# Cross-attention in a decoder layer: exponentials in place, four buffers for the removed scores, queries one step earlier, value products transposed, small operations on GpSimd

## The reference, cut to what matters

```python
q = split_heads(layernorm(x) @ Wq.T + bq)      # 16 heads of 32
k = split_heads(ctx @ Wk.T + bk); v = split_heads(ctx @ Wv.T + bv)
scores = einsum('bhqd,bhkd->bhqk', q, k) / sqrt(32)
top_scores, top_idx = top_k(scores, 32)        # 32 of 722 keys for each query row
w = softmax(top_scores)
out = einsum('bhqk,bhqkd->bhqd', w, v[top_idx])
x = x + out @ Wo.T + bo
```

## Time and profile before

| | |
|---|---|
| time, three runs | 2797.72, 2798.91, 2809.83 us; median 2798.91 |
| span of the profiled execution | 2800.8 us |
| cross-attention, first to last output sum (L1242) | 1206.5 to 2787.4 us |
| busy share of the whole span, PE / DVE / ACT / POOL | 86 / 72 / 50 / 36 % |
| mean granted TensorE clock | 0.88 |

### The profile page before, as it was taken

The page is one execution under the profiler, slowest core; times in us unless marked ns, Lnnn a source line. Parts: engine busy times, 40 slices in busy tenths (PEclk is TensorE's granted clock), DMA queues, the critical chain, the costliest instruction groups (busy, mean ns, idle before and its releaser), DMA issues. The chain is left out here.

```text
span 2800.8 us, 41238 instructions
## 1 busy us (share of the span) xinstructions
PE 2418.1 (86%) x13752; PEld 1992.5 (71%) x13752; DVE 2028.2 (72%) x3897; ACT 1388.0 (50%) x2992; POOL 1016.6 (36%) x912
## 2 busy tenths in 40 slices
PE   3899999999999757898898989888988988988987
PEld 2667767776776536777777868777777877877875
DVE  4544544454454206899898899998989989998996
ACT  3221122112212025667667666766767667676663
POOL 3344334433533112343343343333434433333421
PEclk9787788788878678999999999999999999999987
DMA  4000000000000220010010000000001001000000
GB/s 157 7 18 9 9 17 9 9 9 18 9 9 6 84 86 25 12 28 14 16 28 14 15 20 23 15 20 23 14 16 28 14 16 28 14 16 23 14 1 7
DMA packets 37615, 63.00 MB, mean 22 GB/s; under 512 B 4014, under 2 KB 20542, under 8 KB 37420
## 3 DMA queue, kind: packets, MB, share of 16 engines
q1 hardware_dynamic: 35836, 56.28, 6.7%
q0 software_dynamic: 1584, 4.30, 0.5%
HBM read 53.99 MB, written 6.55 MB: 22 GB/s over the span
## 5 line engine op out<-in xcount | busy, mean ns | idle before, releaser
L1208 DVE MATCH_REPLACE8 ca_W<-ca_top,ca_W 128x722 f32<-128x722 f32 (+1 forms) x624 | 553.5, 894 | 0.0
L1199 DVE MAX8 ca_top<-ca_W 128x8 f32<-128x722 f32 (+1 forms) x624 | 536.4, 898 | 2.6
L855 POOL TENSOR_TENSOR ca_E<-ca_E,ca_S 128x722 f32<-128x722 f32 (+1 forms) x208 | 357.6, 1740 | 308.6 <-ACT ca_S L1060 308.5
L955 PE MATMUL ca_pO<-ca_V,ca_PT 128*128 128x64 f32 (+1 forms) x2496 | 343.1, 293 | 76.8 <-ACT ca_ctxT L1099 76.5
L955 PEld LDWEIGHTS ca_pO<-ca_V,ca_PT 128*128 128x128 f32 (+1 forms) x2496 | 331.1, 205 | 103.8 <-ACT ca_PT L1082 75.6
L837 POOL TENSOR_TENSOR ca_KL<-ca_K,ca_KH 128x384 fp32r<-128x384 f32 (+1 forms) x128 | 114.2, 893 | 496.5 <-ACT ca_KH L1053 496.5
L618 PE MATMUL sa_pq<-sa_V,sa_E 101*100 101x33 f32 x1536 | 258.9, 355 | 29.2 <-POOL sa_E L341 27.8
L618 PEld LDWEIGHTS sa_pq<-sa_V,sa_E 101*100 101x100 f32 x1536 | 257.2, 287 | 30.0 <-issue 30.0
L383 ACT ACTIVATE sa_V<-sa_pp 100x512 f32<-100x512 f32 x48 | 29.2, 608 | 461.1 <-PE sa_pp L90 410.7
L845 POOL TENSOR_TENSOR ca_cL<-ca_raw,ca_cH 128x768 fp32r<-128x768 f32 (+1 forms) x64 | 110.6, 1728 | 332.8 <-ACT ca_cH L1036 332.8
L1187 DVE MAX8 ca_top<-ca_S 128x8 f32<-128x722 f32 (+1 forms) x208 | 181.2, 901 | 54.3 <-ACT ca_S L1077 48.7
(11 more groups left out here) (193 smaller groups left out, 5252.1 us busy)
## 6 DMA issues: line engine op xcount, KB each, us to landing
ca_raw<-in_ctxT SPq DMA_DIRECT2D x32, 384.0 KB, 3.7
ca_raw<-in_ctxT SPq DMA_DIRECT2D x32, 338.0 KB, 3.0
sa_xin<-in_x SPq DMA_DIRECT2D x16, 200.0 KB
sa_xres<-in_x SPq DMA_DIRECT2D x16, 200.0 KB
x_scratch<-sa_x SPq DMA_DIRECT2D x16, 200.0 KB
ca_xin<-x_scratch SPq DMA_DIRECT2D x16, 200.0 KB
out<-ca_x SPq DMA_DIRECT2D x16, 200.0 KB
sa_E<-in_WQ SPq DMA_DIRECT2D x12, 256.0 KB, 13.5
```

The source lines that it names most:

```text
L855: pool.tensor_tensor(E[r][0:t.rows, :], E[r][0:t.rows, :], S[r][0:t.rows, :], ALU.subtract).then_inc(p_ready, 1)
L955: last = pe.matmul(out, PT[:, k, 0:t.rows], rhs, start=k == 0, stop=k == KC - 1)
L1199: n_of[t.i] = order.mark(dve.max(eight, w[rows, :]))
L1208: ins = dve.match_replace(w[rows, :], eight, (w if k else S[r])[rows, :], REMOVED)
```

## The change

All of it is in `cross_program`:

- `exps` writes its exponentials over the scores, in `S`, and so waits until VectorE's first MATCH_REPLACE8 has read them (`removed`); `exps_left` works in `W` in place. `E` is gone, and `W` has four buffers for two.
- The shift (minus the scaled maximum) moves from VectorE to GpSimd (`shifts`, at the head of GpSimd's step, ahead of the subtractions), 1/Z too (`weights`, as a power), and the low part of the queries (`query_low`, at the end of step 5).
- The queries are copied and split by ScalarE at the end of step 5.
- `values` loads 32 columns of V and streams the transposed weights, a block for each head, so that the result stands already transposed in `pO`; a further product writes 1/Z beside it. `normalise`, `output_T` and `place_output` of ScalarE go. In their place ScalarE copies both parts of a group of heads (`keep_output`, five a batch) and GpSimd multiplies them (VectorE for the rest tile, in step 0).
- No work is put off to the next step. y, x2T and f stand behind the first `weights_T`, and the late slices ahead of the first `values`.
- The next batch's x is normalised in step 3 for step 4.

```diff
-        W = [sb(f"W{r}", [128, KV]) for r in range(2)]
+        W = [sb(f"W{r}", [128, KV]) for r in range(RING)]
...
+            def shifts(tb, tp, t):
+                r, rows = ring(t, tp), slice(0, t.rows)
+                pool.wait_ge(peaked, tb.count(NT, t.i + 1))
+                settle(pool)
+                pool.tensor_scalar(shift[rows, r:r + 1], top[r][rows, 0:1], -SCALE, None,
+                                   ALU.mult).then_inc(shift_ready, 1)
...
+                pool.tensor_tensor(S[r][rows, :], S[r][rows, :], W[r][rows, :], ALU.subtract).then_inc(p_ready, 1)
+                need(pool, o_mm, parts_done(ob, Tile(oi)))
+                pool.wait_ge(z_ready, tb.count(NT, t.i + 1))
+                pool.tensor_tensor(rZ[rows, r:r + 1], Z[rows, r:r + 1], minus_one[rows, :], ALU.pow).then_inc(rz_ready, 1)
...
-                if t.i == 0:
-                    pe.wait_ge(q_lo, tb.count(5, 5))
+                if t.i == 0 or t.rest:
+                    pe.wait_ge(q_lo, tb.count(5, 5 if t.rest else 4))
...
+                for _, cols, to, g, q in t.blocks():
+                    pe.matmul(pO[to:to + DH, DEN + at + q.start:DEN + at + q.stop],
+                              rZ[:, r:r + 1].broadcast_to((128, DH)), ident[:, cols], start=True, stop=True)
...
-                    last = pe.matmul(out, PT[:, k, 0:t.rows], rhs, start=k == 0, stop=k == KC - 1)
+                    for _, cols, to, g, q in t.blocks():
+                        last = pe.matmul(pO[to:to + DH, NUM + at + q.start:NUM + at + q.stop],
+                                         V[tp][:, k, 128 * g + to:128 * g + to + DH], PT[:, k, cols],
+                                         start=k == 0, stop=k == KC - 1)
...
             def exps(tb, tp, t):
                 r, rows = ring(t, tp), slice(0, t.rows)
+                act.wait_ge(removed, tb.count(NT, t.i + 1))
+                act.wait_ge(shift_ready, tb.count(NT, t.i + 1))
+                act.activation(S[r][rows, :], S[r][rows, :], ACT.Exp, bias=shift[rows, r:r + 1],
+                               scale=SCALE).then_inc(e_ready, 1)
...
-                                dve.reciprocal(rZ[rows, r:r + 1], Z[rows, r:r + 1]).then_inc(rz_ready, 1)
...
+                        if k == 2 and s == 0 and prev:
+                            dve.wait_ge(ot_ready, b.count(GROUPS, -1))
+                            dve.wait_ge(o_kept, b.count(GROUPS, 0))
+                            rest = [chunks(NR[3 * DH:128, i, 0:4 * REST], 4) for i in range(2)]
+                            dve.tensor_tensor(ctxT[3 * DH:128, :, T - REST:T], rest[0], rest[1],
+                                              ALU.mult).then_inc(ot_ready, 1)
```

More of the change, by code:

```diff
@@ L775, in tiles_at, with parts_done, group_of @@
             return cur, last, coming
[L777 to L781, removed]
+        def parts_done(b, t, before=False):
+            return b.count(PARTS, 2 * t.i if before else min(2 * t.i + 2, PARTS))
+        def group_of(t):
+            if t.rest:
+                return GROUPS - 1
+            return t.g if t.t == 2 else None
         def slices(s, part, b, par, tiles, nxt):
@@ L851, in body @@
                     cur, last, coming = tiles_at(s, b, par, tiles, prev, nxt)
[L852 to L856, removed]
+                    for x in cur:
+                        shifts(*x)
+                    for x in last:
+                        weights(*x)
                     if s == 2 and prev:
@@ new lines, in values @@
+                settle(pe)
+                if t.rest:
+                    n = t.rows
+                    pe.matmul(pO[3 * DH:128, DEN:DEN + n], rZ[0:n, r:r + 1].broadcast_to((n, DH)), ident[0:n, 0:n],
+                              start=True, stop=True)
+                    for g in range(4):
+                        at = NUM + REST * g
+                        for k in range(KC):
+                            last = pe.matmul(pO[3 * DH:128, at:at + REST], V[tp][:, k, 128 * g + 3 * DH:128 * g + 128],
+                                             PT[:, k, REST * g:REST * g + REST], start=k == 0, stop=k == KC - 1)
+                    last.then_inc(o_mm, 1)
+                    return
@@ L967, in body @@
                     cur, last, coming = tiles_at(s, b, par, tiles, prev, nxt)
+                    if coming:
+                        score(*coming[0])
+                    for x in slices(s, 0, b, par, tiles, nxt):
+                        project(*x)
+                    if last:
+                        weights_T(*last[0])
                     if s == 1 and prev:
-                        pe.wait_ge(ot_ready, b.count(NT, 0))
+                        pe.wait_ge(ot_ready, b.count(GROUPS, 0))
                         for c in range(CC):
@@ L1015, in body @@
                         ins.then_inc(q_mm, 1)
-                    if s != 5 and last:
-                        output_T(*last[0])
+                    if len(last) > 1:
+                        values(*last[1])
             each_batch(pe, body)
```

272 lines of the change are left out of this document (129 added, 143 removed).

## The result

The changed kernel takes 2996.19 us (2994.85 to 2996.87), the kernel before on the same chip 2804.37: ratio 1.067, interval 1.0634 to 1.0705. It is slower by 192 us. The profiled execution's span is 2994.4 us, 193.6 more than before.

The account below looks back on a forecast made before the run. VectorE (92% busy) and TensorE (89%) were nearly full, their mutual waits deciding. Steps summed to 115.5 us a batch, 117.0 with clock, 10.2 above 106.8; over 15 batches 2954, so 2952 us, range 2880 to 3030 (55%).

Parts of the forecast that it names:

- VectorE's own pace: VectorE's cross-stage work without waits on other engines, after the change: 93.9 us a batch, about 80% busy.
- The fast rival: VectorE decides because TensorE runs far ahead and old waits vanish: 98.4 us a batch, 2675 us; 17%.
- Where it would wait: VectorE for scores copy (steps 1, 4, 6), f, rest copy; TensorE 4 us each for subtraction (1, 4), query halves (6).
- The steps: Seven parts of a cross-stage batch, 0 to 6; foretold 13.5 to 19.9 us each, sum 115.5.
- The walk: Queue-by-queue timing of a batch's seven steps from VectorE's first MAX8: 115.5 us, 117.0 with the clock, against 106.8 before.
- Clock: TensorE's new idle stretches in steps 1, 4 and 6 lower its clock: 0.5 us each.
- The way into step 4: GpSimd's queue from step 3 into 4: context low part done 3.4, first weights 7.15 us into step 4.
- Values: TensorE's narrow value products: 1.65 us a tile with change-over, 3.0 for the rest tile.
- 106.2 us a batch: Rival that gains and waits cancel: bare pace, half the walk's extra and the clock, 2800 us; 6%.
- the low prices: Rival: the walk with values 1.0, rest 2.55, query halves 0.6, no clock: 111.0 us a batch, 2864 us; 12%.
- GpSimd's prices: Per operation on GpSimd: query half 0.96 us, shift 0.2, power 0.55, subtraction 1.74.
- In-place exponentials at nothing: Exponentials waiting for first replacements delay ScalarE 0.8 us a step, hidden since first weights come later; uncovered, 5.6 a batch.

Follow-up runs that it names:

- e9: Kernel before with four W buffers, exponentials still out of place (E 4, W 4, S 2 buffers): 2801.07 us against 2803.06, ratio 0.9998.
- e5: Changed kernel with the low query halves back on VectorE, in step 6 behind its first replacement: 2943.32 us, ratio 1.0511.
- e3: Changed kernel with y, x2T and f again at the head of TensorE's steps and late slices again behind the second transposition: 2935.67 us, ratio 1.0481.
- e7: Changed kernel with the edits of e3 and e5 together: 2890.06 us, ratio 1.0329.
- e10: Changed kernel with exponentials out of place (E 4, W 4, S 2) and the second scores copy ahead of the second weights copy: 2997.70 us, ratio 1.0687.
- e8: Kernel before with in-place exponentials and four W buffers, nothing else: 2944.81 us, ratio 1.0565.
- e12: e11 with query product in step 4, high halves in step 5, low halves on GpSimd again, second score ahead of first values: 2879.05 us, ratio 1.0245.
- e11: e7 with step 6's first score behind its V slice, several ScalarE and GpSimd reorderings, and exponentials out of place: 2900.29 us, ratio 1.0348.

## Why the prediction held

Forecast 2952 us, measured 2996.19. The mechanism was the one named, and the waits came where they were foretold; that the sum of a batch came within 2 us was in part luck, since errors of several us cancelled. By its steps:

- **VectorE's own pace.** Foretold 93.9 us a batch and 80% busy, measured 93.6 and 79%. The W waits went and the small work went, as priced. None of it reached the time. The fast rival made 98 us of old waits its argument, and half of it has its answer in e9, where the W waits go and the time stays. They were not a cost of their own but the place where VectorE met the pace of the rest. The other half, the waits for the scores copy, grew from 46.8 to 231.7 us.
- **Where it would wait.** Foretold: scores copy in steps 1, 4 and 6, f in 4, rest copy in 0, and on TensorE 4 us each for the subtraction (1 and 4) and the halves (6). Measured: 4.6, 5.3 and 5.15 us on TensorE, and VectorE's waits in the places named; the one small miss is step 4, where f alone does nearly all (3.7 of 4.0 us a batch).
- **The steps.** Foretold 16.8, 17.0, 15.0, 15.1, 19.9, 13.5, 18.2, sum 115.5 and 117.0 with the clock; measured 17.8, 18.9, 15.0, 15.0, 18.4, 12.9, 21.1, sum 119.0. The walk counts from the first MAX8, and step 6 has only one; on its scale steps 5 and 6 took 13.5 and 20.4. Times 15 batches the 2.0 us are 30 of the 40 us by which the profiled execution lies above 2954. Four terms pull against each other in it:
  - *Clock, mis-sized.* I gave 1.5 us a batch. Mean clock fell from 0.95 to 0.90. The lower clock costs the first transposition 0.65 in steps 1 and 4, y 4.70 - 3.05 = 1.65 in step 1, f 0.81 in step 4, the first score 1.96 - 1.1 = 0.86 and the V slice 4.05 - 2.9 = 1.15 in step 6: 5.8 us, and more in the long kind of step 0 (clock 0.70). In step 1 that is 2.3 us, more than the miss of 1.9, in step 6 2.0 of the miss of 2.2.
  - *The stall of the loop, put at nothing.* It is 2.6 to 3.2 us in every second batch, and the walk has no term for it, since its steps were read off a batch that does not have it. So the foretold 16.8 of step 0 is neither the 15.3 of the short kind nor the 21 of the long one, only near their mean.
  - *The way into step 4, mis-sized.* I had GpSimd busy with the context piece until 3.4 and the first weights at 7.15. In the batch shown GpSimd is through with it 0.9 us behind VectorE's first MAX8 of step 4, and TensorE starts the first transposition at 1859.83: 4.7 us into the step, 2.5 earlier than foretold. This is why step 4 came out 1.5 below the walk in spite of the clock.
  - *Values, mis-sized the other way.* 28 passes took 0.97 to 1.32 us where I took 1.65, and the rest tile's 50 passes 1.82 (1922.40 to 1924.22 in TensorE's timeline) where I took 3.0. With five values products and the rest on the chain of the slow steps, my prices were 3 to 4 us a batch too high. This and the way into step 4 hid most of the clock and of the stall. By the Trainium skill, "TensorEngine Tiling (Array Packing)", Overview and Tiling Modes, I had estimated 0.7 to 1.0 with a drain on each side. The trace agrees with strips that run side by side: the time follows the wider of a tile's two blocks (the last section has the numbers). It shows no drain to be priced.
- **Slips in the rivals.** 106.2 us a batch gives 2792 and not 2800, and the low prices as listed take 5.1 off 115.5, which gives 110.4 and not 111.0. Neither moves a rival into another's range.
- **GpSimd's prices.** Halves 4.52 us for four beside 3.84 (1.02 each, with 0.14 between them), shift 0.22 beside 0.2, power 0.56 beside 0.55, subtraction 1.74. The place of the halves was right and its worth is shown: moving them alone takes 53 us off the changed kernel (e5) and 46 off e3 (e7).
- **In-place exponentials at nothing.** Right for the changed kernel as far as e10 shows it, which undoes them, moves one copy as well and does not change the time. But the cover that I named (the first weights come later anyway) was only half of it. e8 shows a second tie that I did not see, of the scores copy to the transposition four tiles before, worth 144 us (2944.81 - 2801.07) in the order of before. The changed kernel hides it, I think, since there the weights copy stands ahead of the scores copy anyway. How much of that order's own cost is owed to making the tie harmless, I can't say: no run has the old order with the new values.
- **How far the cause is shown.** e3 and e5 show two parts, the order of TensorE's work around the first transposition (60 us) and the query halves (53), and e7 that they nearly add up (106). Of the other 86 us, e12 takes some 24 (ratio 1.0245 beside 1.0329; the intervals overlap a little), and its steps 6 and 0 are the ones that are longer than those of before by over 3 us (17.8 and 22.0 beside 14.4 and 15.6); that the rest product and the first scores hold them is read from its trace and not tried. What the low clock costs of each part, apart from the waits that go with it, no run shows. No version that I ran beats the kernel before.

## What to carry to other kernels

A wait that is the longest of an engine is no promise. Ask what comes next at the same pace, and give the engine the buffer alone first, as e9 did. When deferred work is taken out of in-order queues, write down for each first instruction of a step what it now waits for. The 4.5 us of query halves moved onto GpSimd stood ahead of a score and cost some 3.5 us a batch (53 us in 15). An in-place result lengthens the life of its buffer, so look for who writes that slot next. And before a walk starts from the steps of one batch, compare that batch with the mean of all.

## What the runs showed of the hardware

- A tile's values are products with 32-column weights in two blocks on two strips of the array, 28 passes. At the full clock they take 0.97 us where the blocks have 72 and 56 columns to stream, 1.14 with 84 and 44, and 1.32 with 100 and 28. The sum is 128 in all three, so the wider block sets the time: the strips work side by side. An estimate from the three: 0.0125 us a column of the wider block and under 0.1 us for all the rest. The next full-width score starts with no gap behind them (values to 1904.42, score from there).
- The rest tile's 50 passes all go to one strip and take 1.82 us, 0.036 each, against 0.11 for a full-width pass of the kernel before (12 in 1.33).
- GpSimd takes 1.02 us for 32 x 400 elements (four in 4.52), VectorE 0.575 (four in 2.36 in e11). On GpSimd a power of one element per partition takes 0.56 us, a third of a subtraction of 722 columns (1.74), and a multiplication of one element 0.22.
- Steps 1, 4 and 6 of the batch shown have clocks of 0.82, 0.91 and 0.84, which is 6.7, 3.3 and 6.7 us at the 1.2 GHz level, and in each TensorE stood idle for 4.6 to 5.3 us before the first transposition or the first score. The work behind took 2.3, 1.5 and 2.0 us longer than at the full level, so such a wait cost 1.5 to 2.3 us more than its length. e12, with fewer of them, has 0.94.
